# Retention block with quantised FFNs: VectorE's first chains interleaved, one FFN product, Wv's casts and two loads of x moved

## Chip, cores, metric

One Trainium2 chip, 8 cores. Each core computes one of the 8 batch elements by itself (2048 rows of 1024 numbers). The metric is the device time in microseconds of the slowest core.

## What is computed

The weights of the FFN and its input are quantised to a 6-bit grid in blocks of 32; the same FFN stands before and behind a retention layer.

```python
x = x + 0.5 * ffn(layernorm(x), weight, bias)      # out = xd @ wd.T + bias; xd, wd: blocks of 32 on the grid
x = x + attn(layernorm(x), Wq, Wk, Wv, W_G, W_O)
x = x + 0.5 * ffn(layernorm(x), weight, bias)
# attn, per head of 128 (8 heads), gamma_h = 1 - 2**(-5-h):
#   q, k, v = X@Wq, X@Wk, X@Wv
#   ret = ((q @ k.T) / sqrt(128) * gamma**(n-m) for n >= m) @ v;  ret = (ret - mean) * rsqrt(var + 1e-6)
#   out = (silu(X @ W_G) * ret) @ W_O
```

## The kernel before, in words

The rows are worked in 16 chunks of 128. Every engine has its program written out by hand, a fixed order of short steps, and semaphores between them. A chunk c passes through these steps:

- **first FFN**: `st1` (DVE, L439: two bn_stats, L434, and one aggregate, L436), `sm1` (POOL, L1061: four small operations, L1052 to L1058), `xc1` (ACT, L648: x minus its mean), `q1` (DVE, L453: reduce L444, scale L447, reciprocal L448, multiply L449), `xd1` (POOL, L1099, L1105), a transpose, `f1` (PE, 16 matmuls of 128x512, L818), `ev1` (DVE, L471, L474, adds the product to x). `b1` (POOL, L1087, L1091) adds the bias.
- **retention**: `st2`, `sm2` (POOL, L1069), `tn` (ACT, L663, L669), a transpose, then PE makes `proj` k, q, g and v (L893, 16 matmuls each). ACT empties k, q and g (`evK` L685, `evQ` L691, `evG` L699), DVE empties v (`evV` L507, L513). `sc` (PE, L839) forms the scores in P1, `mask` (DVE, L497, L503) cuts them, `ret` (PE, L852) multiplies by v and updates the state, `gn` (DVE, L516, L522 to L526), `smG` (POOL, L1075) and `norm` (ACT, L676, L681) normalise it, `zmul` (DVE, L528, L531), a transpose, `wo` (PE), `evO` (DVE, L481).
- **second FFN**: `st3`, `sm3`, `xc2`, `q2`, `xd2`, a transpose, `f2`, `ev2`, store.

Before the first chunk the FFN's weight has to be quantised and turned. It comes as 8 blocks of 128 rows: `wquant(j)` on DVE (L413: reduce L419, scale L422, reciprocal L424, multiply L427), `wy8(j)` on ACT (L639, L645), `wd(j)` on POOL (L1044, L1048), `wtr(j)` on PE (L916, L908) and `wcp(j)` on ACT (L711, L709). Inside `wquant` each operation waits for the one before it (`step`, L409).

Wk, Wq, Wg, Wv and Wo are loaded and cast to bf16 by POOL's DMA queue (`cast_load`, L1039), two halves each, in that order; x, the FFN's weight and the bias come over SP's queue (L274 on). Transposes of later chunks are DMA transposes, which SP issues too, in its own written order: SP stands still at each wait. There `kt(c)` (L307) waits for `evK(c)` and `sc(c-1)`, `qt(c)` (L313) for `evQ(c)` and `ret(c-1)`.

PE's products go to three pairs of PSUM banks, P0 to P2. `psum_users` (L86) lists who uses which pair in which order; `emptied` (L824) makes PE wait until the pair's last user has been read out. P1 holds `sc` and `ret`, so `sc(1)` waits for all eight parts of `norm(0)`. Around the change the order on PE (L935 to L1012) is:

```python
        f1_half(0, 1); f1(1); xtr(2); f1_half(2, 0)      # turn t0, f1_half(2, 1), proj(0, "k") ...
        ...
        proj(0, "v"); sc(0); proj(1, "v"); ret(0)
        f1(5); proj(2, "k"); proj(2, "q"); sc(1)
        proj(2, "g"); ret(1); wo(0); proj(2, "v")
```

Of the kernel before, what the change touches and what calls it, by code (L numbers as in the profile page):

```python
# [124 lines left out]
def build_program():  # L125
# [280 lines left out]
    def prog_vector(e):  # L406
        own = Tally(sem["v_self"])

        def step(inst):  # L409
            own.up(inst)  # L410
            e.wait_ge(sem["v_self"], own.n)

        def wquant(j):  # L413
# [5 lines left out]
            step(e.tensor_reduce(w_amax[r].unsqueeze(2), b32(wst_sb[j]), AX, ALU.max,  # L419
                                 apply_absolute_value=True))  # L420

            step(e.tensor_scalar(w_scl[r], w_amax[r], 0.5 * R7_5, 0.5 * FLOOR,  # L422
                                 ALU.mult, ALU.max))
            step(e.reciprocal(w_rs[r], w_scl[r]))  # L424
# [28 lines left out]
        def q1(c):  # L453
            p = c % 2
            e.wait_ge(sem["s_xc1"], c + 1)
            if c >= 2:
# [1 line left out]
            if c < 3:
                quant(0, c, xc1_sb[p], x_amax[c], q1_scl[p], x_rs[c], y81_sb[p],
                      "g_sm1", "v_q1")  # L460
            else:
                quant(0, c, xc1_sb[p], q1_amax[p], q1_scl[p], q1_rs[p], y81_sb[p],
                      "g_sm1", "v_q1")
# [68 lines left out]


        wquant(0)
        wquant(1)
        st1(0)
        for j in range(2, 6):
            wquant(j)
        q1(0)
        wquant(6)  # L540
        st1(1)
        wquant(7)
        q1(1)
        st1(2)
        q1(2)
# [92 lines left out]
    def prog_scalar(e):  # L638
        def wy8(j):  # L639
            if j == 0:  # L640
                e.wait_ge(sem["g_const"], 2)
# [82 lines left out]
        for j in range(KC - 1):  # L724
            wy8(j)
            if 2 <= j:
                wcp(j - 2)
            if j == 2:
                xc1(0)
            if j == 4:  # L730
                e.wait_ge(sem["ld_bias"], 16)
                e.activation(bias_sb, bias_sb, AF.Identity, scale=0.5
                             ).then_inc(sem["s_bias"], 1)
        xc1(1)
# [538 lines left out]
```

## Time and profile before

| what | us |
|---|---|
| median of three runs (lowest, highest) | 485.18 (484.07, 485.69) |
| the profiled execution: its own time | 484.67 |
| its span, slowest core (core 2); all cores | 482.8; 479.5 to 482.8 |
| around the span | 1.9 |
| busy on core 2: PE, DVE, POOL, ACT | 432.3, 342.6, 256.4, 190.5 |

PE is busy for 90% of the span, but the page's strip of 40 slices shows that in the first five of them (60 us) it is busy for 0, 2, 2, 6 and 7 tenths, and from then on nearly always for 9. Times of the timeline count from the span's start on core 2. A span is the time from the first to the last instruction of a core; the time of a run has 1.9 us more in it. "Idle before" in square brackets names the engine that was waited for, as it is inferred from semaphores.

### The profile page before, as it was taken

How to read it: one execution, taken by the hardware profiler on the slowest of the kernel's cores; microseconds unless marked ns; L12 is line 12 of the kernel's file. 1: busy time of each engine (PE TensorE's matmuls, PEld its weight loads, DVE VectorE, ACT ScalarE, POOL GpSimd, SP SyncE). 2: the span in 40 equal slices, each digit the busy share in tenths (PEclk: the TensorE clock that was granted, in tenths of full speed). 3: DMA queues.
4: the chain of work that ended last, by engine and by line, in shares of the span. 5: the costliest groups of instructions: out<-in, count | busy, mean ns of one | idle time of the engine just before them, and what ended most of it. 6: DMA issues, size and time to landing. Idle time of an engine off the chain costs nothing.

```text
span 482.8 us, 8182 instructions; the slowest of 8 cores (479.5 to 482.8 us)
## 1 busy us (share of the span) xinstructions
PE 432.3 (90%) x2410; PEld 215.5 (45%) x2456; DVE 342.6 (71%) x656; ACT 190.5 (39%) x270; POOL 256.4 (53%) x328
## 2 busy tenths in 40 slices
PE   0226799999998999999999999999999999999894
PEld 0113354545543535454545445454545454555442
DVE  3886866477888859687786868586947466756782
ACT  1547265236442071607061533426152534614400
POOL 0888765325477554655647464647451624436243
PEclk9999899999999999999999999999999999999999
DMA  7999999974363393635343533645340524233143
GB/s 200 309 182 182 189 157 183 155 116 87 89 110 67 94 208 92 110 67 143 75 133 67 153 68 88 88 88 88 87 81 12 107 45 85 47 67 65 44 153 131
DMA packets 99451, 54.47 MB, mean 113 GB/s; under 512 B 88784, under 2 KB 89040, under 8 KB 99408
## 3 DMA queue, kind: packets, MB, share of 16 engines
q1 hardware_dynamic: 93984, 43.43, 39.5%
q0 software_dynamic: 5280, 10.49, 14.9%
q8 instruction: 20, 0.33, 0.3%
q14 instruction: 23, 0.19, 0.1%
q10 hardware_dynamic: 144, 0.03, 0.0%
HBM read 34.28 MB, written 8.39 MB: 88 GB/s over the span
## 4 chain that ended last, share of the span: by engine, by line
PE 72%; DVE 12%; issue 6%; ACT 3%; DMA 3%; POOL 2%; SPq 1%; DVEq 1%; ACTq 0%; POOLq 0%
PE p L818 64%; DVE p L419 2%; DVE arena L434 2%; PE p L928 2%; DMA arena<-arena 2%; PE pstate L908 1%; PE p L859 1%; DVE arena L444 1%; DMA arena<-wf 1%; PE p L863 1%; PE p L847 1%; ACT arena L709 1%; ACT arena L681 1%; PE pstate L872 1%; DVE arena L522 1%
## 5 line engine op out<-in xcount | busy, mean ns | idle before, releaser
L818 PE MATMUL p<-arena 128*128 128x512 bf16 x1715 | 383.2, 379 | 8.1 <-ACT arena L709 2.7
L818 PEld LDWEIGHTS p<-arena 128*128 128x128 bf16 x1760 | 169.6, 98 | 206.8 <-issue 10.6
L434 DVE BATCH_NORM_STATS2 arena<-arena 128x6 f32<-128x512 f32 x96 | 66.5, 692 | 9.9 <-DVE arena L436 2.2
L669 ACT ACTIVATE arena<-arena 128x1024 bf16<-128x1024 f32 x16 | 19.9, 1243 | 129.1 <-POOL arena L1072 129.1
L1112 POOL TENSOR_TENSOR arena<-arena 128x1024 bf16<-128x1024 fp8e4 x16 | 34.3, 2144 | 46.9 <-DVE arena L449 46.9
L681 ACT ACTIVATE arena<-p,arena 128x128 bf16<-128x128 f32 x128 | 46.4, 473 | 19.2 <-POOL arena L1085 19.2
L444 DVE TENSOR_REDUCE arena<-arena 128x32 f32<-128x1024 f32 x29 | 35.3, 1216 | 19.3 <-ACT arena L660 10.8
L513 DVE TENSOR_TENSOR arena<-p,arena 128x1024 bf16<-128x1024 f32 x16 | 19.6, 1223 | 41.0 <-PE p L818 40.5
L908 PE MATMUL pstate<-arena 128*128 128x128 bf16 x168 | 16.4, 261 | 34.3 <-POOL arena L1048 27.5
L1105 POOL TENSOR_TENSOR arena<-arena 128x1024 bf16<-128x1024 fp8e4 x16 | 30.5, 1909 | 29.3 <-DVE arena L449 26.3
L449 DVE SCALAR_TENSOR_TENSOR arena<-arena 128x1024 fp8e4<-128x1024 f32 x29 | 37.3, 1285 | 3.4 <-DVE arena L448 0.5
L1091 POOL TENSOR_TENSOR arena<-arena 128x1024 f32<-128x1024 f32 x16 | 37.6, 2350 | 3.3 <-ACT arena L653 3.3
L1096 POOL TENSOR_TENSOR arena<-arena 128x1024 f32<-128x1024 f32 x16 | 37.5, 2346 | 0.0
L1052 POOL TENSOR_SCALAR arena<-arena 128x1 f32<-128x1 f32 x48 | 10.7, 224 | 44.6 <-DVE arena L436 43.1
L1082 POOL TENSOR_SCALAR arena<-arena 128x8 f32<-128x8 f32 x16 | 4.0, 250 | 53.8 <-DVE arena L526 53.8
L689 ACT CAST arena<-p 128x1024 bf16<-128x1024 f32 x16 | 16.2, 1014 | 41.1 <-PE p L818 41.1
L908 PEld LDWEIGHTS pstate<-arena 128*128 128x128 bf16 x168 | 13.5, 118 | 39.5 <-issue 38.4
L1053 POOL TENSOR_TENSOR arena<-arena 128x1 f32<-128x1 f32 x48 | 27.3, 570 | 7.1
L709 ACT COPY arena<-pstate 128x1024 bf16<-128x1024 bf16 x21 | 20.9, 1009 | 21.4 <-PE pstate L908 19.0
L503 DVE TENSOR_TENSOR arena<-p,arena 128x1024 bf16<-128x1024 f32 x16 | 19.5, 1220 | 13.2 <-PE p L847 12.9
L522 DVE BATCH_NORM_STATS2 arena<-p 128x6 f32<-128x128 f32 x128 | 26.8, 282 | 2.3 <-PE p L859 2.0
L1084 POOL TENSOR_TENSOR arena<-arena 128x8 f32<-128x8 f32 x16 | 26.8, 1676 | 2.3
(52 smaller groups left out, 397.1 us busy)
## 6 DMA issues: line engine op xcount, KB each, us to landing
arena<-x SPq DMA_DIRECT2D x16, 512.0 KB, 5.3
out<-arena SPq DMA_DIRECT2D x16, 512.0 KB, 2.8
arena<-wf SPq DMA_DIRECT2D x8, 512.0 KB, 11.5
arena<-wk POOLq DMA_DIRECT2D x2, 1024.0 KB, 19.9
arena<-wq POOLq DMA_DIRECT2D x2, 1024.0 KB, 31.5
arena<-wg POOLq DMA_DIRECT2D x2, 1024.0 KB, 40.0
arena<-wv POOLq DMA_DIRECT2D x2, 1024.0 KB, 41.2
arena<-wo POOLq DMA_DIRECT2D x2, 1024.0 KB, 34.0
```

The source lines that it names most:

```text
L434: step(e.bn_stats(bn_ln[:, n, 6 * half:6 * half + 6], x[:, 512 * half:512 * half + 512]))
L444: step(e.tensor_reduce(amax.unsqueeze(2), b32(xc), AX, ALU.max, apply_absolute_value=True))
L449: e.scalar_tensor_tensor(b32(y8), b32(xc), sm[:, n, c, 2:3], bc32(rs), ALU.mult, ALU.mult, saturate=False).then_inc(sem[done], 1)
L522: own.up(e.bn_stats(bn_gn[:, h, :], P1[:, h * 128:(h + 1) * 128]))
L681: e.activation(z_sb[:, h * 128:(h + 1) * 128], P1[:, h * 128:(h + 1) * 128], AF.Identity, scale=gn_a[:, h:h + 1], bias=gn_nb[:, h:h + 1]). ...
L818: last = e.matmul(pair[:, half * 512:half * 512 + 512], lhs[:, kc, :], w[:, kc, half * 512:half * 512 + 512], start=(kc == 0), stop=(kc == ...
L908: last = e.transpose(tb[n % 2][:, kc * 128:(kc + 1) * 128], src[:, kc * 128:(kc + 1) * 128], id_sb)
L1053: step(e.tensor_tensor(sm[:, n, c, 0:1], sm[:, n, c, 3:4], nhalf[:, 0:1], ALU.pow))
L1091: e.tensor_tensor(x_sb[c % XR], x_sb[c % XR], bias_sb, ALU.add).then_inc(sem["g_b1"], 1)
L1096: e.tensor_tensor(x_sb[c % XR], x_sb[c % XR], bias_sb, ALU.add).then_inc(sem["g_b2"], 1)
L1105: e.tensor_tensor(b32(xd1_sb[c % 2]), b32(y81_sb[c % 2]), bc32(q1_scl[c % 2]), ALU.mult).then_inc(sem["g_xd1"], 1)
L1112: e.tensor_tensor(b32(xd2_sb), b32(y82_sb), bc32(q2_scl), ALU.mult).then_inc(sem["g_xd2"], 1)
```

## The change

1. DVE's head is written out anew. `wquant`, `st1` for chunks 0 to 2 and `q1` for chunks 0 to 2 are split into their single operations, and operations of two or three such chains alternate, so that an operation's result is waited for with another chain's operation in between. The number of operations stays.
2. On ACT a small activation at the start loads the table; `xc1`, `wcp` and `xcp` stand in another order.
3. On PE `f1(1)` is cut in halves around `xtr(2)`; `xtr(5)` stands in front of `proj(1, "g")`; `f1(5)` moves from behind `ret(0)` to in front of `proj(0, "v")`; `proj(2, "v")` moves in front of `wo(0)`. The PSUM pairs of these are given out anew.
4. On POOL the second half of Wg moves from behind `wd(5)` to behind `sm1(2)`, both halves of Wv follow, `xd1(2)` stands in front of the second one, `b1` and `sm1` change places here and there.
5. On SP the loads of chunks 6 and 7 of x stand behind `kt(1)` and `qt(1)` and wait until both halves of Wv have landed; before, chunk 6 waited for `proj(1, "k")` and stood in front of `kt(1)`.
6. DVE takes `st1(5)` before `q1(4)`, `ev1(5)` before `evV(0)`, and `evV(2)` before `evO(0)`.

```diff
     order = [("f1", 0, 2), ("f1", 1, 1), ("f1", 2, 0), ("k", 0, 2), ("q", 0, 1),
              ("k", 1, 0), ("f1", 3, 2), ("q", 1, 1), ("g", 0, 0), ("f1", 4, 2),
-             ("g", 1, 1), ("v", 0, 0), ("sc", 0, 1), ("v", 1, 2), ("ret", 0, 1),
-             ("f1", 5, 0), ("k", 2, 2), ("q", 2, 0), ("sc", 1, 1), ("g", 2, 2),
-             ("ret", 1, 1), ("wo", 0, 0), ("v", 2, 2),
+             ("g", 1, 1), ("f1", 5, 0), ("v", 0, 2), ("sc", 0, 1), ("v", 1, 0),
+             ("ret", 0, 1), ("k", 2, 2), ("q", 2, 0), ("sc", 1, 1), ("g", 2, 2),
+             ("ret", 1, 1), ("v", 2, 0), ("wo", 0, 2),
...
         e.wait_ge(sem["v_q1"], 3)
         x_first(5)
-        e.wait_ge(sem["t_k"], 2)
+
+        kt(1)
+        qt(1)
+
+        e.wait_ge(sem["ld_wv"], 32)
         x_first(6)
-
-        kt(1)
         x_first(7)
-        qt(1)
         zt(0)
...
+        def w_max(j):
             e.wait_ge(sem["ld_wf%d" % j], 16)
+            own.up(e.tensor_reduce(w_amax[j % 4].unsqueeze(2), b32(wst_sb[j]), AX, ALU.max,
+                                   apply_absolute_value=True))
+            at["w_max", j] = own.n
+
+        def w_scale(j):
             if j >= 4:
                 e.wait_ge(sem["g_wd"], j - 3)
+            e.wait_ge(sem["v_self"], at["w_max", j])
...
+        w_max(0)
+        w_scale(0)
+        w_max(1)
+        w_recip(0)
+        w_scale(1)
+        w_mul(0)
+        x_st(0, 0)
+        w_recip(1)
+        x_st(0, 1)
+        w_mul(1)
+        w_max(2)
+        x_mean(0)
+        w_scale(2)
+        for j in range(3, 6):
+            w_max(j)
+            w_recip(j - 1)
+            w_scale(j)
+            w_mul(j - 1)
+        x_max(0)
+        w_recip(5)
+        x_scale(0)
+        w_mul(5)
+        w_max(6)
+        x_recip(0)
+        w_scale(6)
+        x_mul(0)
+        x_st(1, 0)
...
+        w_mul(6)
+        w_max(7)
+        x_mean(1)
+        w_scale(7)
+        x_st(2, 0)
+        w_recip(7)
+        w_mul(7)
+        x_max(1)
+        x_st(2, 1)
+        x_scale(1)
+        x_mean(2)
+        x_recip(1)
+        x_mul(1)
+        x_max(2)
+        x_scale(2)
+        x_recip(2)
+        x_mul(2)
         ev1(0)
         st2(0)
         st1(3)
...
         st1(4)
+        st1(5)
         q1(4)
         ev1(3)
-        st1(5)
         q1(5)
         ev1(4)
+        ev1(5)
         evV(0)
         mask(0)
...
         st1(6)
 
-        ev1(5)
         st2(3)
         zmul(0)
         mask(1)
         q1(6)
         st1(7)
         gn(1)
+        evV(2)
         evO(0)
         st3(0)
-        evV(2)
         zmul(1)
...
+        e.wait_ge(sem["g_const"], 2)
+        e.activation(warm, nhalf, AF.Identity, bias=ntie)
+        wy8(0)
+        wy8(1)
+        xc1(0)
+        for j in range(2, 6):
             wy8(j)
+            wcp(j - 2)
+        e.wait_ge(sem["ld_bias"], 16)
+        e.activation(bias_sb, bias_sb, AF.Identity, scale=0.5).then_inc(sem["s_bias"], 1)
+        wcp(4)
+        wy8(6)
         wcp(5)
         xcp(0)
+        xc1(1)
         wy8(7)
         wcp(6)
+        xc1(2)
         wcp(7)
-        xc1(2)
         xcp(1)
         xcp(2)
...
         f1_half(0, 1)
-        f1(1)
+        f1_half(1, 0)
         xtr(2)
+        f1_half(1, 1)
         f1_half(2, 0)
...
         f1(4)
+        xtr(5)
         proj(1, "g")
-        xtr(5)
         e.wait_ge(sem["s_t"], 3)
         turn("t2", t_sb)
+        f1(5)
         proj(0, "v")
 
         sc(0)
         proj(1, "v")
         ret(0)
 
-        f1(5)
         proj(2, "k")
         proj(2, "q")
         sc(1)
         proj(2, "g")
         ret(1)
+        proj(2, "v")
         wo(0)
-        proj(2, "v")
...
         cast_load("wg", 0)
         wd(5)
-        cast_load("wg", 1)
         xd1(0)
         b1(0)
         wd(6)
-        cast_load("wv", 0)
         sm1(1)
         wd(7)
         xd1(1)
         sm1(2)
+        cast_load("wg", 1)
+        cast_load("wv", 0)
+        xd1(2)
         b1(1)
+        sm2(0)
         cast_load("wv", 1)
-        xd1(2)
-        sm2(0)
         b1(2)
         sm1(3)
         sm2(1)
+        xd1(3)
         cast_load("wo", 0)
-        xd1(3)
+        b1(3)
         cast_load("wo", 1)
-        b1(3)
         sm1(4)
         sm2(2)
+        sm1(5)
         b1(4)
         xd1(4)
-        sm1(5)
```

## Rows read from the trace of the kernel before

**Rows 1.** Span and mean granted clock of two of the eight cores.
```profile
core 0: 479.9 us, clock 1.000
core 2: 482.8 us, clock 0.996
```
**Rows 2.** Windows, core 2: length; busy PE, PEld, DVE, ACT, POOL; PEclk, DMA share, GB/s.
```profile
20.80:56.60 35.80, 16.89 (x104) 10.04 (x107) 29.15 (x42) 19.48 (x20) 29.76 (x30) 1.00 1.06 189
...
61.80:111.50 49.70, 49.44 (x288) 24.82 (x291) 30.53 (x51) 23.36 (x29) 23.09 (x29) 1.00 0.91 144
```
**Rows 3.** Waits of POOL, 20.8 to 56.6 us: total, times, longest.
```profile
POOL arena L1048 <- ACT arena L645: 1.4, 2, 1.1
POOL arena L1048 <- PE pstate L908: 1.3, 2, 0.6
POOL arena L1052 <- DVE arena L436: 1.2, 1, 1.2
POOL arena L1105 <- DVE arena L449: 0.8, 1, 0.8
```
**Rows 4.** Timeline of DVE, one block of the weight and the next (start, duration).
```profile
18.90 1.22 DVE L419 TENSOR_REDUCE p<-arena 128x32 f32<-128x1024 f32 x1
20.23 0.19 DVE L422 TENSOR_SCALAR arena<-p 128x32 f32<-128x32 f32 x1
20.52 0.36 DVE L424 RECIPROCAL p<-arena 128x32 f32<-128x32 f32 x1
21.06 1.22 DVE L427 SCALAR_TENSOR_TENSOR arena<-arena,p 128x1024 f32<-128x1024 f32 x1 [0.17 <-DVE p L424]
22.20 1.22 DVE L419 TENSOR_REDUCE p<-arena 128x32 f32<-128x1024 f32 x1
```
**Rows 5.** Timeline of DVE, eight statistics that don't wait for one another.
```profile
100.75 1.68 DVE L522 BATCH_NORM_STATS2 arena<-p 128x6 f32<-128x128 f32 x8 [1.99 <-PE p L859]
```
**Rows 6.** The page's costliest groups: the same line, mean of one.
```profile
L522 DVE BATCH_NORM_STATS2 arena<-p 128x6 f32<-128x128 f32 x128 | 26.8, 282 | 2.3 <-PE p L859 2.0
```
**Rows 7.** The weight's first two blocks, issued at 1.1 and 1.5 us: time to landing.
```profile
DMA to landing us min/median/max: 6.0/6.7/7.4
```
**Rows 8.** Timeline of ACT: the table load.
```profile
10.56 1.28 ACT L645 ACT_TABLE_LOAD   x1 [10.56 <-DVE arena L427]
```
**Rows 9.** Timeline of DVE: the third chunk's reduce and its wait.
```profile
48.46 1.23 DVE L444 TENSOR_REDUCE p<-arena 128x32 f32<-128x1024 f32 x1 [2.39 <-ACT arena L653]
```
**Rows 10.** Timeline of POOL: `sm2(0)` begins.
```profile
55.24 0.22 POOL L1052 TENSOR_SCALAR arena<-arena 128x1 f32<-128x1 f32 x1 [1.16 <-DVE arena L436]
```
**Rows 11.** Timeline of PE: `f1_half(2,0)`, `proj(0,"q")`, `proj(0,"v")`.
```profile
56.30 2.94 PE L928 MATMUL p<-arena 128*128 128x512 bf16 x8 [1.35 <-ACT arena L709]
...
65.77 3.62 PE L818 MATMUL p<-arena 128*128 128x512 bf16 x16
...
92.90 3.40 PE L818 MATMUL p<-arena 128*128 128x512 bf16 x15
```
**Rows 12.** Wq's two halves, issued at 22.7 and 25.6 us: time to landing.
```profile
DMA to landing us min/median/max: 28.8/31.5/34.3
```
**Rows 13.** Wv's second half, issued at 50.6 us: time to landing.
```profile
DMA to landing us min/median/max: 39.2/39.2/39.2
```
**Rows 14.** Loads of chunks 6, 7 and 8 (73.8, 98.2, 120.9 us): 8.6, 6.2, 4.2.
```profile
DMA to landing us min/median/max: 4.2/6.2/8.6
```
**Rows 15.** Timeline of ACT behind `norm(0)`: `xc1(6)`, `evK(2)`.
```profile
108.79 1.18 ACT L653 ACTIVATE arena<-arena 128x1024 f32<-128x1024 f32 x1
109.83 1.05 ACT L689 CAST arena<-p 128x1024 bf16<-128x1024 f32 x1
```
**Rows 16.** Timeline of PE: `ret(0)`, `proj(2,"g")`, and the wait before `f2(1)`.
```profile
100.03 0.61 PE L859 MATMUL p<-arena 128*128 128x128 bf16 x8
...
112.00 3.40 PE L818 MATMUL p<-arena 128*128 128x512 bf16 x15
...
155.84 3.61 PE L818 MATMUL p<-arena 128*128 128x512 bf16 x15 [1.55 <-DMA arena<-arena]
```

More of the change, by code:

```diff
@@ L228, in build_program @@
     ntie = f32at(take(32), 8)[:, 0:1]
+    warm = f32at(take(32), 8)
     wst_sb = [f32at(o_w["wg"] + 4096 * j, D) for j in range(4)] + \
@@ L411, in step @@
             e.wait_ge(sem["v_self"], own.n)
-        def wquant(j):
-            p = j % 2
+        at = {}
+        def w_max(j):
             e.wait_ge(sem["ld_wf%d" % j], 16)
-            r = j % 4
+            own.up(e.tensor_reduce(w_amax[j % 4].unsqueeze(2), b32(wst_sb[j]), AX, ALU.max,
+                                   apply_absolute_value=True))
+            at["w_max", j] = own.n
+        def w_scale(j):
             if j >= 4:
                 e.wait_ge(sem["g_wd"], j - 3)
[L419 to L424, printed above, removed]
+            e.wait_ge(sem["v_self"], at["w_max", j])
+            own.up(e.tensor_scalar(w_scl[j % 4], w_amax[j % 4], 0.5 * R7_5, 0.5 * FLOOR,
+                                   ALU.mult, ALU.max))
+            at["w_scale", j] = own.n
@@ L425, in wquant, with w_recip, w_mul @@
+        def w_recip(j):
+            e.wait_ge(sem["v_self"], at["w_scale", j])
+            own.up(e.reciprocal(w_rs[j % 4], w_scl[j % 4]))
+            at["w_recip", j] = own.n
+        def w_mul(j):
             if j >= 2:
                 e.wait_ge(sem["s_wy8"], j - 1)
-            e.scalar_tensor_tensor(b32(wy_sb[p]), b32(wst_sb[j]), 0.5, bc32(w_rs[r]),
-                                   ALU.mult, ALU.mult).then_inc(sem["v_wy"], 1)
+            e.wait_ge(sem["v_self"], at["w_recip", j])
+            e.scalar_tensor_tensor(b32(wy_sb[j % 2]), b32(wst_sb[j]), 0.5,
+                                   bc32(w_rs[j % 4]), ALU.mult, ALU.mult
+                                   ).then_inc(sem["v_wy"], 1)
@@ new lines, in x_max, with x_scale @@
+        def x_max(c):
+            e.wait_ge(sem["s_xc1"], c + 1)
+            own.up(e.tensor_reduce(x_amax[c].unsqueeze(2), b32(xc1_sb[c % 2]), AX, ALU.max,
+                                   apply_absolute_value=True))
+            at["x_max", c] = own.n
+        def x_scale(c):
+            e.wait_ge(sem["g_sm1"], c + 1)
+            if c >= 2:
+                e.wait_ge(sem["g_xd1"], c - 1)
+            e.wait_ge(sem["v_self"], at["x_max", c])
+            own.up(e.tensor_scalar(q1_scl[c % 2], x_amax[c], sm[:, 0, c, 1:2], FLOOR,
+                                   ALU.mult, ALU.max))
+            at["x_scale", c] = own.n
@@ new lines, in x_recip, with x_mul, x_st @@
+        def x_recip(c):
+            e.wait_ge(sem["v_self"], at["x_scale", c])
+            own.up(e.reciprocal(x_rs[c], q1_scl[c % 2]))
+            at["x_recip", c] = own.n
+        def x_mul(c):
+            e.wait_ge(sem["v_self"], at["x_recip", c])
+            e.scalar_tensor_tensor(b32(y81_sb[c % 2]), b32(xc1_sb[c % 2]),
+                                   sm[:, 0, c, 2:3], bc32(x_rs[c]), ALU.mult, ALU.mult,
+                                   saturate=False).then_inc(sem["v_q1"], 1)
+        def x_st(c, half):
+            if c >= 1 and half == 0:
+                e.wait_ge(sem["v_st1"], c)
+            e.wait_ge(sem["ld_x%d" % c], 16)
+            own.up(e.bn_stats(bn_ln[:, 0, 6 * half:6 * half + 6],
+                              x_sb[c][:, 512 * half:512 * half + 512]))
+            at["x_st", c] = own.n
@@ L430, in stats, with x_mean @@
+        def x_mean(c):
+            e.wait_ge(sem["v_self"], at["x_st", c])
+            e.bn_aggr(mv[:, 0, c, :], bn_ln[:, 0, :]).then_inc(sem["v_st1"], 1)
         def stats(n, c, done):
@@ L440, in st1 @@
             e.wait_ge(sem["ld_x%d" % (c % XR)], 16 * (c // XR + 1))
+            if c == 3:
+                e.wait_ge(sem["v_st1"], 3)
             stats(0, c, "v_st1")
@@ L457, in q1 @@
                 e.wait_ge(sem["g_xd1"], c - 1)
[L458 to L463, printed above, removed]
+            quant(0, c, xc1_sb[p], q1_amax[p], q1_scl[p], q1_rs[p], y81_sb[p],
+                  "g_sm1", "v_q1")
         def q2(c):
@@ L531, in zmul @@
             e.tensor_tensor(z_sb, z_sb, g_sb[c % 2], ALU.mult).then_inc(sem["v_z"], 1)
[L534 to L545, printed above, removed]
+        w_max(0)
[25 more added lines that the diff above has]
+        x_st(1, 0)
+        w_recip(6)
+        x_st(1, 1)
+        w_mul(6)
[15 more added lines that the diff above has]
+        x_mul(2)
         ev1(0)
@@ L639, in wy8 @@
         def wy8(j):
-            if j == 0:
-                e.wait_ge(sem["g_const"], 2)
             e.wait_ge(sem["v_wy"], j + 1)
@@ L723, in prog_scalar @@
         e.dma_start(out=id_sb, in_=id_dr).then_inc(sem["ld_ident"], 16)
-        for j in range(KC - 1):
-            wy8(j)
[L726 to L734, printed above, removed]
+        e.wait_ge(sem["g_const"], 2)
[4 more added lines that the diff above has]
+        for j in range(2, 6):
+            wy8(j)
+            wcp(j - 2)
[3 more added lines that the diff above has]
+        wy8(6)
         wcp(5)
         xcp(0)
+        xc1(1)
         wy8(7)
         wcp(6)
+        xc1(2)
         wcp(7)
-        xc1(2)
         xcp(1)
@@ L754, in prog_scalar @@
         turned("q0", qt_sb)
+        xc1(5)
         tn(2)
@@ L757, in prog_scalar @@
         xcp(4)
-        xc1(5)
         evG(0)
+        xcp(5)
         evG(1)
-        xcp(5)
         e.wait_ge(sem["t_v"], 1)
```

## The prediction

> **What bounds the kernel now.** I looked at the spans of the cores first. The slowest, core 2, takes 482.8 us and had a granted clock a little under 1; core 0, at full clock, takes 479.9 [rows 1]. The windows say where to look: from 61.8 to 111.5 us PE is busy for 49.4 of 49.7 us, and from 20.8 to 56.6 us for 16.9 of 35.8 [rows 2]. So the change can gain only by what it brings forward the point at about 62 us from which PE runs dense, and it keeps that gain only if no new wait arises behind it. In the sparse stretch POOL is busy for 29.8 of 35.8 us and DVE for 29.2; the transfers have all 16 DMA engines taken (share 1.06). POOL's waits there are 1.4 + 1.3 + 1.2 + 0.8 = 4.7 us for other engines, most of it for results that DVE's chain delivers late [rows 3].
>
> **The change, part by part.**
>
> *Alternating chains.* One block of the weight costs DVE 22.20 - 18.90 = 3.30 us [rows 4]. Two big operations of it could follow each other in 1.14 us each (21.06 to 22.20); the reduce holds its follower for 1.33 (18.90 to 20.23), the small ones for 0.29 and 0.54 though they do little. That operations without a wait between them overlap is seen at the eight statistics: 1.68 us for eight [rows 5] whose mean duration is 0.282 [rows 6], so 0.21 each. In the new order each dependent operation has another one in front of it: 1.14 (reduce), up to 0.3 (reciprocal), then the scale, held to 1.33 + 0.1, then the multiply, 0.54 behind the reciprocal, and 1.14 more: about 2.8 us, 0.5 less a block. I bound the saving by 0 and 0.9 (3.30 less two big ones and nothing else) and take 0.5, as the reciprocal's 0.36 remains. The Trainium skill's "VectorE: DVE Perf Modes", section "The DRAIN you can't avoid", says that a next operation doesn't start until the pipe is empty, and that chaining without semaphores saves nothing; by it the saving is 0. The eight statistics don't agree with it; its price is a rival below.
>
> *The first block.* `w_recip(0)` now stands behind `w_max(1)`, which waits for block 1: 1.5 + 7.4 = 8.9 us [rows 7]. Reduce, reciprocal: `w_mul(0)` starts at about 10.6 in place of 9.3, 1.3 later. The table load, 1.28 us [rows 8], used to stand behind it and is now done early. The two cancel: POOL's first cast stays at 15.0.
>
> *POOL becomes the bound of the head.* With DVE 0.5 us a block faster, what POOL waits for is ready. Going through its new order from `wd(2)` at 20.83, I find only some 0.9 us of wait left (for `x_mul(1)` and `x_mul(2)`; the latter's reduce waited 2.39 us for ACT before [rows 9], which `xc1(2)` in front of `wcp(7)` removes). Wv's second cast, 0.8 us of issue, also falls behind `sm2(0)`. So `sm2(0)`, at 55.24 before [rows 10], comes 4.7 - 0.9 + 0.8 = 4.6 us sooner. Wg's and Wv's casts cost POOL the same time in another place.
>
> *PE's head.* `tn(0)`, the turn, `f1_half(2,1)` and `proj(0,"k")` follow `sm2(0)`. `f1_half(2,0)` took 2.94 us for 8 matmuls in this execution [rows 11], about 1.5 us more than half of the 3.6 us for 16: the clock was at its lower level (1.2 GHz) after PE had idled. Core 0 has no such stretch. In the new order that product ends before `t0` can be turned, so such a dip is mostly hidden. PE would be ready for `proj(0,"q")` at about 59.7, before 65.8 [rows 11].
>
> *Wq takes over.* Its second half lands at 25.6 + 34.3 = 59.9 us [rows 12], and POOL's queue holds a backlog: nothing in the change lets Wq come sooner. So `proj(0,"q")` starts at about 60.0: **5.8 us sooner**, and just there the head stops gaining.
>
> *Wv and x.* Wv's second half is issued at 50.6 and lands 39.2 us later, at 89.8 [rows 13]: the time is the queue's backlog, so casts issued some us sooner (Wg's are later, in fact) move nothing. Chunk 6 no longer competes: its load took 8.6 us beside the casts against 4.2 for an undisturbed one [rows 14], so I give Wv 2 us, to about 88 (bounds 0 and 4.4, the difference). V 0 was at 92.9 [rows 11]; with 5.8 us less it would ask at 87.1 and wait; with `f1(5)` in front, 3.6 us (a row of 16), it asks at 90.7. That is covered even if Wv gains nothing.
>
> *What `f1(5)` no longer covers.* It lay between `ret(0)` and `sc(1)` and hid `gn(0)`, `smG(0)` and `norm(0)`, for which `sc(1)` waits since both use P1; behind `norm(0)` ACT has `xc1(6)` and `evK(2)`, and `proj(2,"g")` needs the pair of `evK(2)`. From `ret(0)`'s start at 100.03 [rows 16] to the end of `evK(2)` at 109.83 + 1.05 = 110.9 [rows 15] is 10.9 us. PE came to `proj(2,"g")` after 12.0 us (112.00) [rows 16]; now it would after 12.0 - 3.6 = 8.4. It stalls 10.9 - 8.4 = **2.5 us**, in parts before `sc(1)` and before `proj(2,"g")`. Behind it `proj(2,"v")` waits 0.3 us for `evQ(2)`; this is made good at `f2(1)`, where PE waited 1.55 us for a chain of DVE and a transfer [rows 16]: DVE is helped by `evV(2)` in front of `evO(0)`, which fills a wait for `wo(0)`. `wo(0)` itself has slack.
>
> *x 6 behind `qt(1)`.* `qt(1)` waits for `ret(0)`, at about 98.2, so chunk 6 is issued at 99.6, not 73.8, and chunk 7 0.6 later. With 4.2 to 6.2 us [rows 14] it lands at 103.8 to 105.8; DVE wants `st1(6)` at 102, so DVE stands still for 2 to 4 us, with `st2(3)`, `zmul(0)`, `mask(1)` and `q1(6)` queued behind it. `xc1(6)` then is ready at 106 to 108, where `norm(0)` ends at 106.7: cost 0 to 1.0 us. I take 0, as Wo's transfer should be over by 100 and the undisturbed load is the nearer row.
>
> **Sum.** -5.8 (head) + 2.5 (stall at `sc(1)` and `proj(2,"g")`) + 0.3 - 0.3 = -3.3 us. The profiled execution took 484.67 (span 482.8 and 1.9 around it), so it would take 481.4; the median of the runs, 485.18, is 0.5 above it, and I forecast 481.9 for the median.
>
> **Rivals.**
> - *No overlap on DVE.* If alternating saves nothing, DVE gives back only the 2.39 us of wait and ends `x_mul(2)` at about 49.6 instead of 46.4; `proj(0,"q")` comes at about 62.9, -2.9; with +2.5 and up to 0.8 made good at `f2(1)`: -1.2 us, 484.0. For it: the skill's rule. Against it: the statistics [rows 5, 6]. 10%.
> - *The stall doesn't come.* If `norm(0)`'s chain shrinks because ACT and DVE stand free there, the whole head gain stays: 485.2 - 5.8 = 479.4. Against it: the chain from `ret(0)` had hardly a gap [rows 15, 16]. 12%.
> - *Slower: chunk 6 lands late.* If its load takes 10 us, as under the casts (8.6 [rows 14], and chunk 7 and two transposes are with it), it lands at 109.9; statistics (1.8), `xc1(6)` (1.1) and `evK(2)` (1.0) bring `proj(2,"g")` to 114.1, 2.1 us later than before: 487.3. It decides from a landing at 107.8 on. Against it: Wv and Wo are then over or nearly. 8%.
> - *The clock.* PE's head is sparser, and dips could lie behind `f1_half(2,1)` too: 1.5 us, 483.4 or a little more. 4%, counted as no change.
>
> **How the numbers follow.** The forecast has 66%, with its own range of 480.0 to 483.7 (the unknowns: x 6 up to +1.0, the clock, Wq's landing, which differs by about a us from core to core). A measurement of this kernel tells 0.3% (1.5 us) from no change, so faster begins below 483.7. Faster: 66 + 12 = 78%. Same: 10 + 4 = 14%. Slower: 8%. The range from 479.3 to 484.6 leaves out the slow rival and the ends of the others.
>
> **What would show it.** Right: the table load at about 1 us; DVE's block at 2.8 us; POOL without waits from 21 to 52 us; `proj(0,"q")` at 60 on most cores, right behind Wq's landing; V 0 at 90 to 91 without a wait; PE idle for some 2.5 us between `ret(0)` and `proj(2,"g")`, named after ACT; `st1(6)` waiting for a DMA. Wrong: a block still at 3.3 us (first rival); `proj(2,"g")` more than 5 us sooner (second); x 6 landing after 107 (third); PE's rows of 16 longer than 3.6 us behind 50 us (fourth).

## The result: slower by 0.75% where a gain of 0.7% was forecast

The changed kernel takes 488.89 us (median of four runs, 488.61 to 489.52), the kernel before 484.91 beside it: a ratio of 1.0075, 95% interval 1.0055 to 1.0095. The forecast was 481.9, with a range to 484.6. Executions in which the cores of one die ran at a lower clock and some per cent longer are left out of every ratio and interval, though not of the medians, so where the two differ the ratio counts. Its profiled execution took 489.52 us, with a span of 487.7 on core 5. On its page PE is busy for 437.7 us, 5.4 more than before; DVE with 343.0, POOL with 257.3 and ACT with 191.5 are each within 1.0 us of before.

The spans of all cores of the changed kernel, with the mean granted clock:

```profile
core 0: 485.2 us, clock 1.000
core 1: 484.1 us, clock 0.995
core 2: 484.1 us, clock 0.999
core 3: 486.6 us, clock 0.992
core 4: 485.9 us, clock 0.993
core 5: 487.7 us, clock 0.985
core 6: 485.9 us, clock 0.987
core 7: 487.4 us, clock 0.987
```

Each core is slower than core 2 was before [rows 1], so it is no accident of one core; and the longest go with the lowest clock. The same two windows as in [rows 2], core 5:

```profile
20.80:56.60 35.80, 21.59 (x123) 11.73 (x124) 27.68 (x42) 19.85 (x20) 30.72 (x29) 0.90 1.05 191
61.80:111.50 49.70, 46.88 (x280) 23.51 (x280) 25.49 (x44) 19.89 (x26) 20.82 (x23) 1.00 0.84 140
```

In the stretch that was dense PE is now busy for 46.9 of 49.7 us instead of 49.4. The timeline of PE shows where (start, duration; in brackets the idle time before and who ended it): `proj(0,"q")`, `ret(0)`, `proj(2,"k")` with `proj(2,"q")`, `sc(1)`, `proj(2,"g")`, and `f2(1)` and a later product.

```profile
62.50 3.62 PE L906 MATMUL p<-arena 128*128 128x512 bf16 x16
...
100.76 0.61 PE L947 MATMUL p<-arena 128*128 128x128 bf16 x8
...
101.65 7.12 PE L906 MATMUL p<-arena 128*128 128x512 bf16 x32
109.79 0.61 PE L935 MATMUL p<-arena 128*128 128x128 bf16 x8 [1.02 <-ACT arena L766]
113.84 5.69 PE L906 MATMUL p<-arena 128*128 128x512 bf16 x16 [3.44 <-ACT arena L774]
...
154.94 3.61 PE L906 MATMUL p<-arena 128*128 128x512 bf16 x16 [1.04 <-DMA arena<-arena]
...
172.38 0.81 PE L906 MATMUL p<-arena 128*128 128x512 bf16 x3 [1.57 <-DVE arena L537]
```

Against [rows 11, 16] this makes a ledger. `proj(0,"q")` starts 3.3 us sooner than on core 2 of before (62.50, 65.77). `proj(2,"g")` starts some 2 us later (113.84; the row of before shows 112.00 with 15 matmuls, as one record is missing): the gain is gone and more, in two stalls of 1.02 and 3.44 us. And behind the second one 16 matmuls take 5.69 us in place of the 3.62 of every undisturbed row of 16, another 2.1 us: the granted clock is 0.50 from 113.84 to 117.00 us, the lower of its two levels (1.2 GHz in place of 2.4). The mean clock of 0.985 comes from such rows, here and in the head (0.90 in the first window). All waits of PE behind 61 us add up to 12.4 us here and 5.8 on core 2 before. 0.7 of them lie ahead of `proj(0,"q")`, so -3.3 + (12.4 - 5.8 - 0.7) + 2.1 = +4.7 us, against 487.7 - 482.8 = +4.9.

Where the 3.44 comes from is told by DVE's and ACT's timelines of the same execution. DVE: `evV(1)`, `st1(6)`, `st2(3)`, `zmul(0)`, `mask(1)`. ACT: `norm(0)`, `xc1(6)`, `evK(2)`.

```profile
103.81 1.19 DVE L566 TENSOR_TENSOR arena<-p,arena 128x1024 bf16<-128x1024 f32 x1
109.70 1.49 DVE L489 BATCH_NORM_STATS2 arena<-arena 128x6 f32<-128x512 f32 x2 [4.69 <-DMA arena<-x]
...
111.74 1.49 DVE L489 BATCH_NORM_STATS2 arena<-arena 128x6 f32<-128x512 f32 x2 [0.24 <-DVE arena L491]
...
113.79 2.43 DVE L584 TENSOR_TENSOR arena<-arena 128x1024 bf16<-128x1024 bf16 x1 [0.24 <-DVE arena L491]
116.14 1.21 DVE L556 TENSOR_TENSOR arena<-p,arena 128x1024 bf16<-128x1024 f32 x1
```

```profile
106.74 2.90 ACT L766 ACTIVATE arena<-p,arena 128x128 bf16<-128x128 f32 x8 [3.82 <-POOL arena L1174]
111.65 1.15 ACT L738 ACTIVATE arena<-arena 128x1024 f32<-128x1024 f32 x1 [2.00 <-DVE arena L491]
112.70 0.99 ACT L774 CAST arena<-p 128x1024 bf16<-128x1024 f32 x1
```

Chunk 6 of x is late. DVE stands still for 4.69 us, ACT's `xc1(6)` for 2.00 us behind it, and `evK(2)`, which has nothing to do with chunk 6 but stands behind `xc1(6)` on ACT, frees PE's pair only at 113.7. The loads of chunks 6 and 7, their own rows (issue of the first and last; time to landing):

```profile
L282 SPq DMA_DIRECT2D arena<-x x2: 432/470/507, 102.8 to 103.3; - x2
...
DMA to landing us min/median/max: 6.8/7.1/7.4
```

102.8 + 6.8 = 109.6, when DVE goes on. It isn't so on all cores. `proj(2,"g")` of cores 0, 3 and 6:

```profile
111.48 3.61 PE L906 MATMUL p<-arena 128*128 128x512 bf16 x16 [1.33 <-ACT arena L774]
...
112.63 5.30 PE L906 MATMUL p<-arena 128*128 128x512 bf16 x16 [1.42 <-ACT arena L774]
...
112.12 5.04 PE L906 MATMUL p<-arena 128*128 128x512 bf16 x16 [1.33 <-ACT arena L774]
```

There the wait is 1.33 to 1.42 us, though chunk 6 is late there too (DVE waits 1.82 to 2.67 us for it), and yet on cores 3 and 6 the clock falls. (Cores 1, 5 and 7 wait 1.79, 3.44 and 2.85; cores 2 and 4 1.33 and 1.66.)

### The profile page after: what moved, and what is told of

Read it like the earlier page. It is cut to its first block, busy times and chain, and to the rows that moved or that the text cites. A ratio compares the mean times of both kernels' runs of the same rounds, so it can differ in the third digit from the quotient of the medians.

```text
span 487.7 us, 8227 instructions; the slowest of 8 cores (484.1 to 487.7 us)
## 1 busy us (share of the span) xinstructions
PE 437.7 (90%) x2456; PEld 215.7 (44%) x2456; DVE 343.0 (70%) x656; ACT 191.5 (39%) x271; POOL 257.3 (53%) x328
## 4 chain that ended last, share of the span: by engine, by line
PE 68%; DVE 9%; DMA 7%; issue 6%; POOL 4%; ACT 3%; SPq 2%; DVEq 0%; POOLq 0%; ACTq 0%
PE p L906 62%; DMA arena<-x 7%; DVE arena L489 2%; ACT arena L766 2%; PE p L935 1%; PE p L947 1%; POOL arena L1194 1%; PE p L951 1%; PE pstate L960 1%; DVE arena L501 1%; DVE arena L547 1%; SPq L277 1%; POOL arena L1180 1%; DVE arena L575 1%; PE pstate L996 1%
## 5 line engine op out<-in xcount | busy, mean ns | idle before, releaser
L489 DVE BATCH_NORM_STATS2 arena<-arena 128x6 f32<-128x512 f32 x90 | 62.3, 693 | 14.8 <-DMA arena<-x 4.7
L566 DVE TENSOR_TENSOR arena<-p,arena 128x1024 bf16<-128x1024 f32 x16 | 19.6, 1223 | 35.6 <-PE p L906 35.2
L506 DVE SCALAR_TENSOR_TENSOR arena<-arena 128x1024 fp8e4<-128x1024 f32 x29 | 38.8, 1336 | 3.0
L527 DVE TENSOR_TENSOR arena<-p,arena 128x1024 f32<-128x1024 f32 x16 | 19.5, 1218 | 12.9 <-PE p L906 11.9
## 6 DMA issues: line engine op xcount, KB each, us to landing
arena<-wo POOLq DMA_DIRECT2D x2, 1024.0 KB, 30.1
```

What stands on the lines that cost most here:

```text
L489: step(e.bn_stats(bn_ln[:, n, 6 * half:6 * half + 6], x[:, 512 * half:512 * half + 512]))
L506: e.scalar_tensor_tensor(b32(y8), b32(xc), sm[:, n, c, 2:3], bc32(rs), ALU.mult, ALU.mult, saturate=False).then_inc(sem[done], 1)
```

## Experiments

Two theories, with the letters that the expectations use. A: the late chunk 6 costs what the slow rival said. B: `f1(5)` in front of V 0 leaves a stall behind `ret(0)` that is dearer than forecast. And for the head, which gained less than 5.8 us: what took the gain. Ratios are to the kernel before, run on the same chip (its medians 484.5 to 484.7).

### 1. The two loads put back in front of `kt(1)`; `f1(5)` put back; both

The first kernel leaves the loads behind Wv but in front of the transposes:

```diff
+        e.wait_ge(sem["ld_wv"], 32)
+        x_first(6)
+        x_first(7)
         kt(1)
         qt(1)
-
-        e.wait_ge(sem["ld_wv"], 32)
-        x_first(6)
-        x_first(7)
```

> The changed kernel with one thing different: the loads of chunks 6 and 7 still wait for both halves of Wv, but stand in front of kt(1) and qt(1) on SP, so they no longer wait for sc(0) and ret(0). Theory A (the late chunk 6 is the price: in the changed kernel it lands at 109.6 us on the slowest core, DVE stands still for 4.7 us before st1(6), and mask(1) and proj(2,g) come late): chunk 6 is issued at about 88 and lands before 96, st1(6) no longer waits, mask(1) comes at 111 in place of 116, and 3 to 4.5 us come back: 484.5 to 486. Theory B (the price is f1(5), which no longer covers norm(0)): DVE's wait goes, but the stalls before sc(1) and proj(2,g) stay: at most 1 us comes back, 488.

The second puts `f1(5)`, its pairs and `ev1(5)` back and leaves the loads late:

```diff
-        f1(5)
         proj(0, "v")
...
         ret(0)
+        f1(5)
         proj(2, "k")
...
-        ev1(5)
         evV(0)
...
         st1(6)
+        ev1(5)
         st2(3)
```

> The changed kernel with f1(5) back behind ret(0) (with its PSUM pairs, and ev1(5) back behind st1(6)); the two loads stay behind kt(1), qt(1) and Wv. Theory A: ret(0) comes 3.5 us sooner, and with it qt(1) and chunk 6, so a part comes back, 1 to 2.5 us: 486.5 to 488; st1(6) still waits for its transfer. Theory B: the stalls before sc(1) and proj(2,g), 2.4 us on most cores, and the fall of the clock behind them go: 3 to 4 us, 485 to 486. proj(0,v) may wait up to 1.5 us for Wv in both.

The third does both. In it and in the second `proj(2,"v")` still stands in front of `wo(0)` and `evV(2)` in front of `evO(0)`.

> Both at once: f1(5) back behind ret(0), and the two loads behind Wv but in front of kt(1). If A and B each carry a part, this is the best of the four, 2 to 3 us below the kernel before: 482 to 483. If the head of the change gains nothing, it comes out at the kernel before, 485, or a wait for Wv in front of proj(0,v) (1 to 2 us) shows that f1(5) was needed there.

Measured: 487.67 us, 1.0060 (1.0043 to 1.0077); 486.94, 1.0059 (1.0029 to 1.0089); 483.70, 0.9985 (0.9972 to 0.9998). Against the changed kernel's 1.0075 the loads alone bring 0.0015 (0.7 us, less than the intervals can tell), `f1(5)` alone 0.0016 (0.8), and both together 0.0090 (4.4). By these three alone it looks as if two delays of like length hid each other; the fourth kernel, below, shows that they don't. PE of the first kernel, core 1: `sc(1)`, `proj(2,"g")`, `proj(2,"v")`.

```profile
110.06 0.61 PE L934 MATMUL p<-arena 128*128 128x128 bf16 x8 [1.02 <-ACT arena L765]
112.00 3.61 PE L905 MATMUL p<-arena 128*128 128x512 bf16 x16 [1.33 <-ACT arena L773]
...
118.01 6.20 PE L905 MATMUL p<-arena 128*128 128x512 bf16 x28 [1.06 <-ACT arena L781]
```

With chunk 6 in time the wait is 1.33 on every core, and 1.02 + 1.33 + 1.06 = 3.4 us of pure theory B are left; against the third kernel, where these waits are gone on all cores, the price is 1.0060 - 0.9985 = 0.0075, 3.6 us (4.0 by the medians). The second kernel against the third is 1.0059 - 0.9985 = 0.0074, again 3.6 us (3.2 by the medians), but that is not the price of the late chunk in the changed kernel. In the second kernel, core 5, DVE and then PE:

```profile
104.17 1.49 DVE L489 BATCH_NORM_STATS2 arena<-arena 128x6 f32<-128x512 f32 x2 [3.00 <-DMA arena<-x]
...
106.22 1.23 DVE L527 TENSOR_TENSOR arena<-p,arena 128x1024 f32<-128x1024 f32 x1 [0.24 <-DVE arena L491]
```

```profile
107.59 5.18 PE L906 MATMUL p<-arena 128*128 128x512 bf16 x16 [2.66 <-DVE arena L527]
```

`ev1(5)` stands behind `st1(6)` here, while the changed kernel has it in front, so putting `f1(5)` back has opened a new path: the late chunk holds PE's `proj(2,"q")`, by 2.66 us and by 5.18 - 3.62 = 1.6 us more at the lower clock. Not every such stall brings the lower clock; core 0 of the same execution:

```profile
107.84 3.61 PE L906 MATMUL p<-arena 128*128 128x512 bf16 x16 [2.71 <-DVE arena L527]
```

To see that this is the path, one more, the fourth kernel of this section, takes the second one's late loads and only puts `ev1(5)` in front of `st1(6)`:

```diff
+        ev1(5)
         st1(6)
-
-        ev1(5)
```

> As the run with f1(5) back behind ret(0) (x 6 and 7 still late), but ev1(5) stands in front of st1(6) on DVE, so that PE's wait for the pair of f1(5) in front of proj(2,q) (2.7 us in that run) no longer hangs on chunk 6. If that wait and the fall of the clock behind it are the way in which the late chunk 6 reaches PE, the time falls from 486.9 to 484 to 485; what is left is DVE's own lateness (zmul(0), mask(1), q1(6)). If the late chunk acts through mask(1) and evK(2) alone, it stays at 486.5 to 487.

Measured: 485.09, 1.0009 (0.9994 to 1.0023), 1.9 us less than with `ev1(5)` behind (2.4 by the ratios). PE then has 48 matmuls in one row where it had stood (core 5, 98.83 to 109.2). The load is as late as ever (landed at 104.2 us on core 5, 104.0 in the second kernel); most of what it cost went through the instruction queued behind it.

This is the kernel that tells the two theories apart, as it takes `f1(5)` out of the changed kernel without the new path. `f1(5)` is worth 1.0075 - 1.0009 = 0.0066, 3.2 us, with the loads late, and 3.6 with them in time. The late loads are worth 1.0009 - 0.9985 = 0.0024, 1.2 us, with `f1(5)` back, and 0.7 with it forward. Each pair agrees within its interval (some 0.002 on each difference), so the two prices add up as far as these runs can tell, and `f1(5)` is the larger by far.

### 2. The same two parts put into the kernel before

One moves only the loads of chunks 6 and 7 behind `qt(1)`, with the wait for Wv:

> The kernel before with one thing of the change: the loads of chunks 6 and 7 stand behind kt(1) and qt(1) and wait for Wv. ret(0) ends at 100.6 there, so chunk 6 is issued at about 102 and lands at 107 to 109; st1(6) was taken at 104.2. Theory A (a late chunk 6 costs by itself): DVE waits 3 to 5 us at st1(6), ev1(5) and mask(1) stand behind it, proj(2,q) waits for ev1(5), and the time rises by 2.5 to 4 us to 487 to 488.5. Rival (it costs only together with the moved f1(5)): 484.5 to 485.5.

The other moves only `f1(5)` in front of V 0, with its pairs, `xtr(5)`, `xcp(5)` and `ev1(5)`:

> The kernel before with one thing of the change: f1(5) in front of proj(0,v), with its PSUM pairs, xtr(5), xcp(5) and ev1(5) moved as that needs; all loads as before. Theory B (f1(5) covered norm(0), and without it PE stands still before sc(1), proj(2,g) and at the pair behind them): 3 to 4 us of waits between ret(0) and wo(0), 487.5 to 488.5. Rival (the prediction's sum, 2.5 us, with part given back): 486 to 487. If Wv bound the kernel before, which its trace doesn't show, it would gain: 484.

Measured: 489.71, 1.0103 (1.0083 to 1.0123), and 492.72, 1.0161 (1.0139 to 1.0183). Each alone costs the kernel before 5 and 8 us, more than was expected of either. The first, core 0, DVE and PE:

```profile
106.92 1.49 DVE L434 BATCH_NORM_STATS2 arena<-arena 128x6 f32<-128x512 f32 x2 [4.46 <-DMA arena<-x]
...
108.97 1.23 DVE L474 TENSOR_TENSOR arena<-p,arena 128x1024 f32<-128x1024 f32 x1 [0.24 <-DVE arena L436]
```

```profile
99.10 7.12 PE L818 MATMUL p<-arena 128*128 128x512 bf16 x32
110.34 6.08 PE L818 MATMUL p<-arena 128*128 128x512 bf16 x16 [4.12 <-DVE arena L474]
```

4.12 + (6.08 - 3.62) = 6.6 us at one place of that core, for a load that is issued at 100.2 and needs 6.5 us. Here too `ev1(5)` stands behind `st1(6)`, as in the second kernel of section 1. The second, core 6, PE: `xtr(5)` and what follows, then `sc(1)`, `proj(2,"g")` and `wo(0)`, which takes over the pair of `proj(2,"q")` in this kernel as `proj(2,"v")` does in the changed one.

```profile
90.37 1.01 PE L908 MATMUL pstate<-arena 128*128 128x128 bf16 x8 [2.27 <-POOL arena L1105]
91.17 4.79 PE L818 MATMUL p<-arena 128*128 128x512 bf16 x16
...
116.08 0.61 PE L847 MATMUL p<-arena 128*128 128x128 bf16 x8 [1.02 <-ACT arena L681]
118.02 3.61 PE L818 MATMUL p<-arena 128*128 128x512 bf16 x16 [1.33 <-ACT arena L689]
...
124.03 4.26 PE L818 MATMUL p<-arena 128*128 128x512 bf16 x19 [1.06 <-ACT arena L697]
```

The stall behind `ret(0)` has the same three parts to the hundredth, 3.4 us, in a kernel with the old head: it is the price of the place of `f1(5)`, with either head. The other 2.27 us, and 0.4 + 1.2 at the lower clock (1.01 for 0.61, 4.79 for 3.62), are not: POOL's `xd1(5)` isn't ready so early in the order of before, and the change had moved `st1(5)` up for that.

### 3. The head alone

The changed kernel with loads, `f1(5)`, `evV(2)`, and the order of `proj(2,"v")` and `wo(0)` as before; what is left of the change are DVE's alternating chains, ACT's and POOL's new order and `f1(1)` in halves:

> Only the head of the change (alternating chains, the order of ACT, of POOL and of the first products); f1(5), proj(2,v) behind wo(0), evV(2) and the loads of chunks 6 and 7 as in the kernel before. Theory of the prediction (the head brings the dense part 2 to 6 us forward): proj(0,q) at 60 to 63, and 1.5 to 3 us below the kernel before, 482 to 483.5, with a wait for Wv in front of proj(0,v). Rival (the head gains nothing on the slowest cores, because chunk 2's load blocks DVE and the clock is at its lower level): 485.

Measured: **482.78, 0.9952 (0.9936 to 0.9968)**, by the ratio 2.3 us less than before, and the fastest kernel here: it beats both the kernel before and the changed one. It also beats the third kernel of section 1, which shares its head, by 0.9985 - 0.9952 = 0.0033 or 1.6 us: what is left of the change there, the loads' wait for Wv, `proj(2,"v")` in front of `wo(0)` and `evV(2)` in front of `evO(0)`, costs as well. Which of the three it is wasn't taken apart. Its `proj(0,"v")` waits for nothing, so `f1(5)` wasn't needed as a cover for Wv. DVE, core 6, one block of the weight in the new order (reduce, reciprocal, scale, multiply, and the next reduce), and POOL's waits from 20.8 to 56.6 us (total, times, longest):

```profile
16.37 1.22 DVE L421 TENSOR_REDUCE p<-arena 128x32 f32<-128x1024 f32 x1
17.50 0.35 DVE L436 RECIPROCAL p<-arena 128x32 f32<-128x32 f32 x1
17.76 0.17 DVE L430 TENSOR_SCALAR arena<-p 128x32 f32<-128x32 f32 x1
17.95 1.22 DVE L443 SCALAR_TENSOR_TENSOR arena<-arena,p 128x1024 f32<-128x1024 f32 x1
19.09 1.22 DVE L421 TENSOR_REDUCE p<-arena 128x32 f32<-128x1024 f32 x1
```

```profile
POOL arena L1194 <- DVE arena L469: 1.6, 2, 0.9
```

19.09 - 16.37 = 2.72 us a block, where [rows 4] had 3.30; a block whose multiply still waits for its scale takes 3.07 (20.68 to 23.75 on core 5 of the changed kernel). The next kernel is this one with DVE's operations in their old, sequential order and nothing else changed:

> The head-only kernel of the last runs with DVE's operations in the order of before, each waiting for the one in front of it; the orders of ACT, POOL, PE as in the changed head. If the alternating chains carry the head's gain, a block of the weight takes 3.3 us again, POOL waits 4 to 5 us for DVE and the gain is gone: 484.5 to 485.5. If the gain comes from the orders of ACT and POOL, it stays at 482.8 to 483.3.

Measured: 485.20, 1.0013 (0.9998 to 1.0028). POOL's waits, core 6:

```profile
POOL arena L1122 <- ACT arena L715: 2.5, 3, 1.6
POOL arena L1122 <- PE pstate L981: 1.7, 3, 0.6
POOL arena L1179 <- DVE arena L469: 1.3, 2, 0.8
```

5.5 us of waits in place of 1.6, and `proj(0,"q")` at 65.39 in place of 62.75. So the alternation carries the whole gain of the head (2.4 us by the medians, 3.0 by the ratios, 2.6 at `proj(0,"q")`), and the rest of the new order brings nothing without it. The size is less sure than the sign: the two kernels ran on different chips, and the first kernel of section 4, nearly the head-only one, run on the chip of the sequential one, is 1.0013 - 0.9976 = 0.0037 or 1.8 us ahead of it.

### 4. What holds the head at 2 us

Chunk 2's statistics in front of `w_recip(7)` wait for a load on some cores (1.21 us on core 5 of the changed kernel). The first kernel puts them behind `w_mul(7)` and `x_max(1)`:

> The head-only kernel with both halves of chunk 2's statistics behind w_mul(7) and x_max(1), so that chunk 2's transfer, which lands at 29 to 35 us depending on the core, no longer holds the last block of the weight. If that wait is why some cores gain less in the head, their first turn (t0) comes 0.5 to 1.2 us sooner and the slowest core with it: 482.0 to 482.5. If POOL alone sets the head, nothing changes: 482.8.

Measured: 483.45, 0.9976 (0.9960 to 0.9991): no gain on 482.78. The wait isn't on the path, or what is gained is lost behind it. The second finishes the weight's first block before the second is touched, since `w_recip(0)` waits for block 1 in the new order:

```diff
         w_max(0)
         w_scale(0)
-        w_max(1)
         w_recip(0)
-        w_scale(1)
         w_mul(0)
+        w_max(1)
+        w_scale(1)
```

> The head-only kernel with the first block of the weight finished (reduce, scale, reciprocal, multiply) before the second block's reduce, which waits for its transfer. In the changed head POOL's first cast is issued 8.4 to 9.0 us after the first block's landing, in the kernel before 7.85. If that 0.8 us lies on the head's path, t0 and the time fall by 0.5 to 0.8 us, to 482.0 to 482.3. If other waits take it up: 482.8.

Measured: 1.0000 (0.9971 to 1.0030), and scattered, from 481.95 to 488.49 us. The first of Wk's casts is issued at 11.7 us on core 1, 2 us earlier than in the changed kernel, as wanted (13.9 on core 5 there); on all eight cores it comes 6.56 us behind the first reduce, where the kernel before needed 7.85. Six of the eight cores come to 477.5 to 480.2 us, a little below the head-only kernel's 478.0 to 481.0, but core 1 takes 486.4 and core 3 483.1. Core 1, DVE, and chunk 1's and 2's loads (issued 6.9 and 7.7 us):

```profile
37.02 0.69 DVE L477 BATCH_NORM_STATS2 arena<-arena 128x6 f32<-128x512 f32 x1 [6.94 <-DMA arena<-x]
```

```profile
DMA to landing us min/median/max: 7.3/30.1/32.7
```

Chunk 0's load lands in 7.3 us, the two next in 30.1 and 32.7; on core 5 of the changed kernel chunk 2 took 27.6. The bias, issued at 6.4, takes 27.1. That the casts of POOL's queue, let go earlier, take the DMA engines from SP's loads that are still under way is a likely reason and not shown: on core 4 the first cast is issued at 11.0 us, earlier still, and the two loads take 22.0 and 25.3. What is shown is that they differ from core to core (20.3 to 32.7 us over the eight), and the metric is the slowest of eight.

The third fills PE's gaps between `xtr(0)` and `xtr(1)` with 40 small products, which keep it busy and add nothing to the result, once on the head-only kernel and once on the one with the first block first:

> The head-only kernel with 40 small products of the identity with itself, written to a pair of banks that is not yet in use, in PE's gaps between xtr(0) and xtr(1). They add work and nothing else. If PE's lower clock in f1_half(0,1) and f1_half(1,0) (4.5 to 6.1 us for 16 matmuls where 3.6 is usual) delays ev1(0) and with it sm2(0) and t0, these take 3.6 us again and the time falls by 0.3 to 1.0 us. If the lower clock there is hidden behind POOL: 482.8, or 0.3 more where the added work stands in the way.

> Both of the last two changes on the head-only kernel: first block finished first, and PE kept busy in its gaps. If both terms lie on the path they add up: 481.3 to 482.0, the fastest of all. If POOL's queue alone sets the head, it equals the run with the first block alone.

Measured: 483.34, 0.9977 (0.9964 to 0.9990), and 484.55, 1.0001 (0.9973 to 1.0029). No gain, and the second kernel is not the fastest, as it would be if the two terms added up. The test is weaker than it looks, though. In the first kernel the 16 matmuls behind `xtr(1)` do take 3.62 us on cores 0, 3 and 6 (4.73, 4.69 and 4.53 head-only), but the 16 behind `xtr(2)`, 3.62 before, now stand behind a wait of 2.2 us for POOL and take 4.92 to 5.30. The granted clock of core 0 is 1.00 from 34 to 46 us and 0.83 from 46 to 56 (0.89 and 0.96 head-only): the dip moved and didn't go. Whether the lower clock in the head is hidden stays open.

## Why the prediction was wrong, by its steps

By parts; each measured size is a difference of two ratios to the kernel before, times 484.6 us, and good to some 1 us:

| part | forecast | measured | from |
|---|---|---|---|
| the head | -5.8 | -2.3 | head-only kernel |
| `proj(2,"v")` in front of `wo(0)`, `evV(2)`, loads behind Wv | 0 | +1.6 | third kernel of section 1, against head-only |
| loads behind `kt(1)`, `qt(1)` | 0 | +1.2 | fourth kernel of section 1, against the third |
| `f1(5)` | +2.5 + 0.3 - 0.3 | +3.2 | changed kernel, against the fourth |
| sum | -3.3 | +3.7 | |

**Right.** DVE's block (2.8 forecast, 2.72 measured), and so the weight of the statistics against the rule of the Trainium skill: by "The DRAIN you can't avoid" ("VectorE: DVE Perf Modes") the gain between the two kernels of section 3 would be nothing, and it is 1.8 to 3.0 us. The same page's section "Two Vector instructions with no wait between them" makes only a held instruction wait for every earlier one to finish; the trace agrees with that one (0.35 us reciprocal from 17.50, scale from 17.76). V 0 without a wait (Wv's second half is issued at 53.9 on core 5 and has landed by 88); the idle time of PE named after ACT; `st1(6)` waiting for a DMA; the table load out of the way (at 1.54 us).

**Wrong: the head, -5.8 us.** This is the largest miss, 3.5 us. It measured 2.3 us as a kernel of its own, and over the eight cores `proj(0,"q")` starts a mean of 1.5 us sooner in the changed kernel. The steps that were off:
- It was counted from core 2's 65.8 us, the latest of the eight cores, which has a stretch at the lower clock [rows 11]; the others start that product at 62.2 to 64.2. "Such a dip is mostly hidden" brought nothing on the five cores that had none. The mean of the eight was 63.8, so 2.0 of the 4.3 us that are missing in the mean are this: the slowest core's own time was taken for that of all.
- "Only some 0.9 us of wait left" for POOL: it is 1.6 for chunks 1 and 2 (and 1.5 more for `wy8` on core 5). So `sm2(0)`, forecast 4.6 us sooner, at 50.6, begins at 52.41 on core 5 and at a mean of 52.2, 2.0 us sooner than the mean of before. That is another 1.6 us of the 4.3.

```profile
52.41 0.22 POOL L1141 TENSOR_SCALAR arena<-arena 128x1 f32<-128x1 f32 x1
```

- "Wq takes over": it doesn't. Wq lands at 59.3 to 61.2 us, near the forecast of 59.9, but `proj(0,"q")` starts 0.1 to 3.1 us behind that, and the turn in front of it waits 0.72 us for `tn(1)`, which hangs on POOL, on every core (61.0 and 62.50 on core 5). These 0.7 are the rest.
- "The two cancel" for the first block: on seven of the eight cores the first cast comes later behind the first reduce than before, 8.4 to 9.0 us instead of 7.85, as `w_max(1)` waits for its block (0.94 us on core 6 of the head-only kernel).

**Wrong: what `f1(5)` no longer covers, +2.5 us, and +0.3 - 0.3.** The mechanism is right and the two waits that it counts are well sized: 1.02 + 1.33 = 2.35 us where nothing disturbs them, with the kernel before's own order too (section 2). But the next user of the pair of `proj(2,"q")` waits 1.06 us, not 0.3, where the clock hasn't fallen (1.06 to 1.29 on seven cores of section 1's first kernel), and nothing is given back at `f2(1)`: PE waits 1.04 us there instead of 1.55 and then 1.57 for `evO`. Measured, the term is 3.2 to 3.6 us. It outweighs the whole gain of the head, so it alone makes the sign: with chunk 6 in time the kernel is still 0.6% slower than before (first kernel), without it 0.15% faster (third).

**Wrong: the rest of the order, at nothing.** It costs 1.6 us, and the sum has no term for it: "`wo(0)` itself has slack", `evV(2)` was to help, and for the loads the sum counts only the place behind `qt(1)`. No run shows which of them costs.

**Wrong: chunk 6, 0 of 0 to 1.0 us.** It costs 0.7 to 1.2 us. On core 5, the slowest, its path came as the slow rival, given 8%, had written it: a landing at 109.6, beyond its point of 107.8, and `proj(2,"g")` at 113.84 (rival: 114.1). That the two numbers agree is luck: the rival had the issue at 99.6 and a load of 10 us, and it was 102.8 and 6.8. The issue is late since `ret(0)` started at 100.8 and not at 98.2, so an error of the head went into this term too. The load itself was within or near the forecast's 4.2 to 6.2 us on most cores (3.6 to 6.8 over the eight); on core 5 the two errors pass the rival's point only together (99.6 + 6.8 = 106.4, 102.8 + 4.2 = 107.0).

**Not in the sum at all: the clock behind a stall.** The rival of the clock looked for dips in the head only, though its sign, rows of 16 longer than 3.6 us behind 50 us, came true. They came behind the new stalls in the dense part: 5.69, 6.21, 5.18, 6.08 and 4.79 us for 16 matmuls that take 3.62. All eight stalls of 2.8 to 4.2 us in the traces of the changed kernel, of the second kernel of section 1 and of section 2's first have such a row behind them; behind shorter ones some cores have it and some don't (2.66 us and 5.18 on core 5 of the second kernel, 2.71 and 3.61 on core 0). It is partly taken back: in the changed kernel `proj(2,"v")` doesn't wait on the five cores where `proj(2,"g")` is slow, and waits 0.67 to 1.77 us on the three where it isn't.

What stays open: how much of each part is clock on which core, which of the three smaller moves costs the 1.6 us, and which of POOL's waits limits the head-only kernel now. Wq's landing is not its limit on core 6: 58.9 us, and `proj(0,"q")` starts at 62.75.

## What to carry to other kernels

A product that covers a chain of other engines is worth its cover, not its place: before it is moved, work out what the chain needs, add every follower that shares a pair of banks with it, and count that a stall of 2 to 4 us may cost as much again for the clock (0 to 2.8 us here; the most, 6.44 in place of 3.62, behind 3.31 us on core 7 of section 2's first kernel). A load that is put behind a late point costs through whatever stands behind its reader on that engine's queue, so put the urgent, independent operation ahead (`ev1(5)` in front of `st1(6)`: 1.9 us). When one part of a change is put back to price it, look in the trace for a wait that the new mixture has made: the second kernel of section 1 priced `f1(5)` at 0.8 us, and without its own new wait it is 3.2. And read the gain of a head on all cores before taking the slowest core's as the kernel's.

## What the hardware showed that I had not expected

- After PE idled 2.27 us its next 16 matmuls took 4.79 us, after 2.66 us 5.18, after 2.85 us 6.21, after 3.44 us 5.69, after 4.12 us 6.08, where 3.62 is the rule, with a granted clock of 0.50 in the first 3.2 us behind the stalls of 3.44 and 4.12: a stall can cost more than its own length, and how much doesn't follow the length. After 2.71 us on another core they took 3.61. Two waits of 1.02 and 1.33 us some 2 us apart brought it on core 6 of the changed kernel (5.04) and not on core 0.
- Two loads of 512 KB issued half a us apart, with no weights under way, land in 3.6 and 4.3 us on core 2 and in 6.8 and 7.4 on core 5 of the same execution.
- A load of SP's queue that is issued at 7 to 8 us took 30.1 and 32.7 us on one core and 20.7 and 23.7 on another of the same execution, beside casts of POOL's queue, against 7.3 and 8.2 for the load ahead of them.
